# Stacked remainder rows in the product with V, other instruction orders in the attention blocks, and FFN input rows transposed on VectorE with six PSUM banks at the end of a pair

## The chip, the cores and the metric

The kernel runs on one core of one Trainium2 chip. The metric is the device time in microseconds of one launch. The kernel before takes 872.28 us (median of 3 runs, 872.03 to 872.45).

## The reference

A gated block of 2 x 2048 tokens of width 512: cross-attention to 77 context tokens per batch (16 heads of width 32), then an FFN of hidden width 1536 with integer weights, each behind a layer norm and a tanh gate. Cut to what matters:

```python
q = (layernorm(x) @ Wq.T);  k = ctx @ Wk.T;  v = ctx @ Wv.T          # 16 heads, 32 wide
scores = einsum('bhqd,bhkd->bhqk', q, k) * 32 ** -0.5
scores = where(arange(sq)[:, None] >= arange(77)[None, :], scores, -1e9)
x = x + tanh(g_xattn) * (softmax(scores) @ v) @ Wo.T
n = layernorm(x)
h = silu(n @ (w_gate / 127).T) * (n @ (w_up / 127).T)                 # 1536 wide
x = x + tanh(g_ffn) * h @ (w_down / 127).T
```

All arrays are fp32. The products run in fp32r with operands split into a high part (a copy rounded to fp32r) and a low part (the rest), so that a product of two split operands is three matmuls (high-high, low-high, high-low).

## The kernel before, in words

The 4096 rows are 8 blocks (`n`) of 512, each of 4 tiles (`t`) of 128 rows. Every engine has its own instruction list, written out by hand; semaphores alone tie the lists together, and nothing is reordered by a scheduler.

**Phase 1, attention.** A step handles one block. TensorE (PE) computes the queries transposed (`query`), per tile the scores (two units of 8 heads, 616 columns each, `score_unit`), transposes the probabilities (`transpose_p`, 10 transposes of 128 columns per tile, in three groups `r` of 4, 4 and 2), multiplies them with V (`values`, one block late), and projects with Wo (`project`). ScalarE (ACT) takes the exponentials (`exp0`, `exp1`) and writes the high parts (`p_high`, `m_high`, `x_high_t`); VectorE (DVE) takes maxima and sums, and writes the low parts (`p_low`, `m_low`); GpSimd (POOL) multiplies with the reciprocal denominators (`weigh`) and writes low parts of x (`x_low_t`). Loops over `n` are hardware loops. The 308 keys of a group of 4 heads are two chunks of 128 rows and a remainder of 52. In a unit of two groups the remainders lie side by side in one chunk of 104 rows, which both groups use, each with zero rows in V for the other. So a group has 3 chunks with 3 matmuls each: 9 matmuls of 512 columns, 4 groups per block.

**Phase 2, FFN.** Blocks go in 4 pairs (`p`). Gate and up projections of a pair are a Strassen-like scheme: for each of 12 slices `m` of the hidden width seven products `p1` to `p7` of 4 matmuls each (`strassen`, stationary operand from `ring`, moving operand from `xv`). The moving operands are the four quarters of the normalised, transposed input (B11, B12, B21, B22) and four differences T1 to T4. For pair 0 they are made at the end of phase 1. For every later pair they are made at the end of the pair before: PE transposes the rows (`turn`, 4 x 8 transposes) into PSUM, ACT rounds (`xv_copy`, `xv_high`), DVE forms differences and low parts (`form`, `xv_low`), POOL the low parts of T1 to T4. In each slice ACT snapshots partial sums from PSUM (`snap1` to `snap3`), takes tanh, and DVE makes silu of it (`silu1`, `silu2`) and the hidden values. POOL writes the low part of the hidden values (`h_low`). The down projection (`down`, 8 tiles of 12 matmuls) comes in two halves: the first after slice 6, the second at the pair's end. It writes two PSUM banks in turn (`m_bank`), and DVE adds each tile to `acc` (`result`). DVE takes row statistics and normalises the next pair's rows during the first half of the down projection (`first_half`). The last products of a pair are `p4(last)` and `p3(last)`, which wait for ACT's and DVE's treatment of `p7(last)`.

## Time and profile before

| what | us |
|---|---|
| median of 3 runs | 872.28 |
| the profiled execution, whole | 872.86 |
| its span | 871.0 |
| PE busy | 855.0 (98%) |
| DVE busy | 653.3 (75%) |
| ACT busy | 461.1 (53%) |
| POOL busy | 403.1 (46%) |

The granted TensorE clock stands at its full level in all 40 slices of the page. A row of a timeline names the start, the duration, the engine, the source line, the operation with output and inputs, its shape, and how many of them were merged. Matmuls overlap, so the pace of a run of matmuls is the distance from its start to the start of the next run, over its count, and not the mean duration. Idle time before a row stands in brackets, with what ended it.

### The profile page before, as it was taken

The numbers are of one execution on the slowest core, as the hardware profiler recorded it, in microseconds if no ns is written. First come the engines' busy times: TensorE is split into PE (matmuls) and PEld (weight loads), VectorE is DVE, ScalarE is ACT, GpSimd is POOL, SyncE is SP. The second block draws the span as 40 slices with busy tenths as digits, with TensorE's granted clock in tenths as the row PEclk, the third lists the DMA queues.
The fourth block names the chain that finished last, engine by engine and source line by source line (L and its number), as shares of the span: only waits on it lengthen the run. The fifth ranks groups of instructions, "written<-read, shape, count | busy, mean of one in ns | idle before, by whom it ended". The sixth has DMA issues, their size and how long they took to land.

```text
span 871.0 us, 12870 instructions
## 1 busy us (share of the span) xinstructions
PE 855.0 (98%) x4087; PEld 706.8 (81%) x4087; DVE 653.3 (75%) x1081; ACT 461.1 (53%) x1130; POOL 403.1 (46%) x344
## 2 busy tenths in 40 slices
PE   8999999999999999999999999999999999999997
PEld 6678888888888887888888888888888888888876
DVE  5988877777786878679688478788487887587882
ACT  5787575756666757546056265165363364461550
POOL 4664555555565665437144444155253256151250
PEclk9999999999999999999999999999999999999999
DMA  9233847272728131567333256043275143243202
GB/s 329 78 107 121 270 153 253 84 241 85 242 97 277 48 133 38 212 234 266 116 120 135 97 187 248 14 165 122 74 247 187 48 164 107 96 171 117 90 38 98
DMA packets 60406, 128.73 MB, mean 148 GB/s; under 512 B 7616, under 2 KB 20416, under 8 KB 60352
## 3 DMA queue, kind: packets, MB, share of 16 engines
q1 hardware_dynamic: 58960, 125.95, 41.9%
q10 hardware_dynamic: 1392, 2.10, 0.7%
q8 instruction: 29, 0.48, 0.2%
q14 instruction: 25, 0.20, 0.1%
HBM read 99.93 MB, written 27.79 MB: 147 GB/s over the span
## 4 chain that ended last, share of the span: by engine, by line
PE 86%; DVE 6%; ACT 3%; issue 1%; DMA 1%; POOL 1%; ACTq 0%; DVEq 0%
PE psum L1880 34%; PE psum L1591 20%; PE psum L1930 18%; PE psum L1660 9%; PE psum L1616 4%; DMA xs<-x_t 1%; PE psum L1704 1%; ACT e L800 1%; POOL hT L705 1%; DVE bn L1055 1%; DVE K L1149 1%; DVE mx L1105 1%; DVE e L1097 0%; DVE qT L1079 0%; DVE mx L1094 0%
## 5 line engine op out<-in xcount | busy, mean ns | idle before, releaser
L1880 PE MATMUL psum<-xv,ring 128*128 128x512 f32 x1344 | 308.0, 390 | 1.0 <-ACT a L985 0.7
L1880 PEld LDWEIGHTS psum<-xv,ring 128*128 128x128 f32 x1344 | 251.3, 188 | 55.1 <-ACT a L985 1.1
L705 POOL TENSOR_TENSOR hT<-th,hT 128x512 fp32r<-128x512 f32 x48 | 86.7, 1806 | 200.7 <-ACT hT L1005 200.7
L1930 PE MATMUL psum<-w_d,hT 128*128 128x512 f32 x768 | 177.7, 390 | 1.3 <-POOL hT L705 0.8
L1930 PEld LDWEIGHTS psum<-w_d,hT 128*128 128x128 f32 x768 | 143.6, 188 | 32.7 <-POOL hT L705 2.0
L554 POOL TENSOR_TENSOR e<-e,rden 128x616 f32<-128x616 f32 x64 | 78.0, 1219 | 110.4 <-DVE rden L1131 75.2
L800 ACT ACTIVATE e<-psum,nmx,q_scale 128x77 f32<-128x77 f32 x256 | 102.9, 428 | 3.1 <-DVE nmx L1111 3.1
L973 ACT ACTIVATE a<-psum 128x512 f32<-128x512 f32 x48 | 28.7, 599 | 131.6 <-PE psum L1880 131.4
L1471 DVE SCALAR_TENSOR_TENSOR acc<-psum,gate_ffn,acc 128x512 f32<-128x512 f32 x64 | 47.6, 749 | 65.1 <-PE psum L1930 65.1
L1660 PE MATMUL psum<-wo,aT 128*128 128x512 f32 x384 | 95.5, 398 | 0.5 <-DVE aT L1079 0.5
L1591 PE MATMUL psum<-xT,wq 128*128 128x512 f32 x360 | 89.1, 398 | 0.4 <-DVE qT L1079 0.4
L1660 PEld LDWEIGHTS psum<-wo,aT 128*128 128x128 f32 x384 | 69.8, 188 | 14.3 <-DVE aT L1079 0.8
L1591 PEld LDWEIGHTS psum<-xT,wq 128*128 128x128 f32 x360 | 65.5, 188 | 14.7 <-DVE qT L1079 1.9
L705 POOL TENSOR_TENSOR hT<-c,hT 128x512 fp32r<-128x512 f32 x48 | 62.3, 1297 | 22.2 <-ACT hT L1005 22.2
L1591 PE MATMUL psum<-pT,V 128*128 128x512 f32 x288 | 68.0, 392 | 0.6 <-DVE aT L1079 0.6
L773 ACT ACTIVATE pT<-psum 128x512 fp32r<-128x512 f32 (+1 forms) x96 | 49.7, 534 | 33.9 <-PE psum L1616 33.9
L1591 PE MATMUL psum<-K,qT 128*128 128x308 f32 x384 | 63.9, 310 | 0.9 <-ACT e L800 0.9
L1591 PEld LDWEIGHTS psum<-pT,V 128*128 128x128 f32 x288 | 53.3, 188 | 12.5 <-DVE aT L1079 1.1
L1435 DVE SCALAR_TENSOR_TENSOR th<-th,c 128x512 f32<-128x512 f32 x48 | 56.1, 1168 | 7.1 <-ACT th L998 4.3
L1591 PEld LDWEIGHTS psum<-K,qT 128*128 128x128 f32 x384 | 56.9, 188 | 5.4 <-ACT e L800 1.8
L1005 ACT ACTIVATE hT<-th 128x512 fp32r<-128x512 f32 x48 | 30.4, 633 | 54.2 <-DVE th L1448 54.2
L1068 DVE TENSOR_TENSOR pT<-psum,pT 128x512 fp32r<-128x512 f32 (+1 forms) x96 | 55.7, 588 | 2.6 <-ACT pT L773 0.9
(110 smaller groups left out, 1204.7 us busy)
## 6 DMA issues: line engine op xcount, KB each, us to landing
ring<-w_var SPq DMA_DIRECT2D x48, 896.0 KB, 4.6
w_var<-stage SPq DMA_DIRECT2D x12, 896.0 KB, 4.6
x_ln<-x SPq DMA_DIRECT2D x32, 256.0 KB, 4.7
x_res<-x SPq DMA_DIRECT2D x32, 256.0 KB, 5.2
x_mid<-x_res SPq DMA_DIRECT2D x32, 256.0 KB, 2.0
x<-x_mid SPq DMA_DIRECT2D x16, 512.0 KB, 5.6
acc<-x_mid SPq DMA_DIRECT2D x16, 512.0 KB, 6.2
out<-acc SPq DMA_DIRECT2D x32, 256.0 KB, 2.0
```

The lines of the kernel that those rows point to most:

```text
L554: nc.gpsimd.tensor_tensor(e[:, t % 2, hs], e[:, t % 2, hs], rden[:, t % 2, hs].unsqueeze(2).to_broadcast([P, UH, SK]), ALU.mult).then_inc( ...
L705: nc.gpsimd.tensor_tensor(hT[:, 1, i % HH, j, :], h[:, :], hT[:, 0, i % HH, j, :].bitcast(f32), ALU.subtract).then_inc(h_lo, 1)
L773: nc.scalar.activation(dst, src, ACT.Copy).then_inc(t_hi, 1)
L800: last = nc.scalar.activation(e[:, t % 2, UH + h, :], s_bank[1][:, h // HG, (h % HG) * SK:(h % HG + 1) * SK], ACT.Exp, bias=nmx[:, t % 2, ...
L1068: nc.vector.tensor_tensor(dst, src, hi.bitcast(f32), ALU.subtract).then_inc(t_free, 1)
L1435: nc.vector.scalar_tensor_tensor(th2[:, :], th2[:, :], 1.0, c22[:, :], ALU.add, ALU.mult)\
L1471: nc.vector.scalar_tensor_tensor(acc[:, t, :], m_bank[t % 2][:, :], gate_ffn[:, 0:1], acc[:, t, :], ALU.mult, ALU.add).then_inc(m_free, 1)
L1591: last = nc.tensor.matmul(dst, stat, mov, start=(j == 0), stop=(j == len(terms) - 1))
L1616: last = nc.tensor.transpose(t_bank[at % 2][:, j * P:(j + 1) * P], rows[:, start:start + P], ident[:, :])
L1660: last = nc.tensor.matmul(m_bank[t % 2][:, :], aT[:, a, m, t * P:(t + 1) * P], wo[:, c, m, :], start=m == 0 and a + c == 0, stop=m == G - ...
L1880: last = nc.tensor.matmul(psum[:, bank, :], stat, mov, start=start and j == 0, stop=j == len(terms) - 1, skip_group_check=not start)
L1930: last = nc.tensor.matmul(m_bank[t % 2][:, :], hT[:, a, m, t // TT, (t % TT) * P:(t % TT + 1) * P], w_d[:, HH * h + m, :], start=m == 0 an ...
```

## The change

**Attention.** A remainder of 52 rows is now kept in 64 partitions. The low part of the same rows goes to the other 64 partitions of the same operand `pR`, and V holds its remainder rows twice. One matmul with V's high part then does high-high and high-low, one with V's low part does the rest: 8 matmuls per group in place of 9. The transposes are regrouped: `r` = 0 and 1 are the four full chunks of unit 0 and of unit 1, `r` = 2 the two remainders. For `r` = 2 ACT and DVE have two instructions on 64 partitions each in place of one on 128. The orders of ACT, DVE and POOL within a step are others. All four groups' remainder matmuls wait for the last low part of the block before (`t_base(n)`).

**FFN.** For pairs 1 to 3 PE transposes nothing. POOL normalises the rows in slices 2, 3 and 5; DVE takes the statistics in slices 1 to 4 and transposes the rows in 32 instructions per pair (`turn_rows`, each 16 blocks of 32 x 32, all from one group of 32 partitions into another), of which 20 lie between the results of the first half of the down projection (`FILL`), 3 ahead of them and 9 in slices 7 to 9. The differences and low parts read SBUF in place of PSUM; T1 and T3 are formed in slices 10 and 11. ACT computes Silu itself, and DVE's `silu1` and `silu2` are gone. At a pair's end the second half of the down projection uses six PSUM banks (the two of `m_bank` and four of the products'), and `p4(last)` and `p3(last)` stand between parts of its first three tiles. The row maxima of the weights (`largest_gu`) are all taken in the last pair, where before 6 slices' were taken in the first.

`values_full` waits for `t_free` of `split - 2 + m // 2` and has 2 chunks of 3 matmuls; `values_rest` waits for `split` and has the 2 matmuls with `pR`. The two loops over `odd` are those of `p_high` and `p_low` for `r` = 2.

```diff
-    SH = 2 * (GK - 2 * P)
-    CS = [0, P, 2 * P, 2 * P + SH, 3 * P + SH]
+    HP = P // 2
+    CS = [0, P, GK - HP, HK - 2 * P, HK - P]
...
             def values(i, m, b, split):
-                pe.wait_ge(t_free, split)
-                m_wait(i)
-                product(m_bank[m % 2][:, :],
-                        [(V[:, B - 1 - b, a, 3 * m + c, :], pT[:, d, CU * (m // 2) + 2 * (m % 2) + c, :])
-                         for c in range(3) for a, d in CROSS]
-                        ).then_inc(m_full, 1)
+                values_full(i, m, b, split)
+                values_rest(m, b, split)
...
+                for odd in range(2):
+                    rows = slice(odd * HP, odd * HP + HP)
+                    last = nc.scalar.activation(pR[rows, :, odd, c], src[rows], ACT.Copy)
...
+                for odd in range(2):                                              # p_low, r = 2
+                    last = nc.vector.tensor_tensor(pR[other, :, odd, c], src[rows], pR[rows, :, odd, c].bitcast(f32),
+                                                   ALU.subtract)
...
+            def turn_rows(q, half_of, ops):
+                tiles = slice(TT * half_of, TT * half_of + TT)
+                dve.wait_ge(x2_normed, PT * q + TT * (half_of + 1))
...
+                for op in ops:
+                    a, c = divmod(op, HG)
+                    rows = x2[a * HD:(a + 1) * HD, tiles, :].rearrange("p t (k n) -> p t k n", n=P)
+                    to = x2_t[half_of][c * HD:(c + 1) * HD].rearrange("p k (t n) -> p t k n", n=P)
+                    nc.vector.transpose(to[:, :, :, a * HD:(a + 1) * HD], rows[:, :, :, c * HD:(c + 1) * HD])\
+                        .then_inc(x2_turned, 1)
...
-                nc.scalar.activation(th1[:, :], psum[:, set_a[i % 2], :], ACT.Tanh, scale=0.5 * W_SCALE)\
-                    .then_inc(tanh1_done, 1)
+                nc.scalar.activation(th1[:, :], psum[:, set_a[i % 2], :], ACT.Silu, scale=W_SCALE)\
+                    .then_inc(silu1_done, 1)
...
+            def down_bank(h, t):
+                bank = {2: set_c[0], 3: set_b[1], 4: set_c[1], 5: set_a[1]}
+                return psum[:, bank[t], :] if h and t in bank else m_bank[t % 2][:, :]
...
-                if more:
-                    turn(p + 1, B11)
-                    turn(p + 1, B12)
+                early, late = range(HH - 2), range(HH - 2, HH - 1)
+                down(p, 1, 0, early)
                 p4(last)
+                down(p, 1, 1, early)
                 p3(last)
-                down(p, 1, 0, range(HH - 1))
-                down(p, 1, 1, range(HH - 1))
+                down(p, 1, 2, early)
+                for t in range(3):
+                    down(p, 1, t, late)
```

PE's instructions at the end of a pair that is not the last, of the kernel before. L1880 are the Strassen products, L1704 the transposes of `turn`, L1930 the down projection:

```order
L1930 MATMUL psum<-w_d,hT 128x512 x96
L1880 MATMUL psum<-xv,ring 128x512 x140
L1704 MATMUL psum<-ident,x 128x128 x16
L1880 MATMUL psum<-xv,ring 128x512 x8
L1930 MATMUL psum<-w_d,hT 128x512 x24
L1704 MATMUL psum<-ident,x 128x128 x16
L1930 MATMUL psum<-w_d,hT 128x512 x72
```

The same place of the changed kernel, where L1982 are the products and L2042 the down projection:

```order
L2042 MATMUL psum<-w_d,hT 128x512 x96
L1982 MATMUL psum<-xv,ring 128x512 x140
L2042 MATMUL psum<-w_d,hT 128x512 x8
L1982 MATMUL psum<-xv,ring 128x512 x4
L2042 MATMUL psum<-w_d,hT 128x512 x8
L1982 MATMUL psum<-xv,ring 128x512 x4
L2042 MATMUL psum<-w_d,hT 128x512 x80
```

The 32 transposes are gone, and 8 matmuls of the down projection stand ahead of each of the last two products.

DVE's instructions in the second part of the first half of the down projection, of the kernel before: L1471 is `result`, L1257 and L1259 are the statistics, L1265 the normalisation, L1421 and those behind it belong to the next slice:

```order
L1471 SCALAR_TENSOR_TENSOR acc<-psum,gate_ffn,acc 128x512
L1257 BN_STATS bn<-x 128x6
L1259 BN_AGGR mv<-bn 128x2
L1471 SCALAR_TENSOR_TENSOR acc<-psum,gate_ffn,acc 128x512
L1265 TENSOR_SCALAR x<-x,mv,rstd 128x512 x2
L1257 BN_STATS bn<-x 128x6
L1259 BN_AGGR mv<-bn 128x2
L1471 SCALAR_TENSOR_TENSOR acc<-psum,gate_ffn,acc 128x512
L1265 TENSOR_SCALAR x<-x,mv,rstd 128x512 x6
L1421 TENSOR_TENSOR c<-psum,a 128x512
L1435 SCALAR_TENSOR_TENSOR th<-th,c 128x512
L1441 SCALAR_TENSOR_TENSOR th<-th,psum 128x512
```

And of the changed kernel, where L1567 is `result` and L1362 `turn_rows`:

```order
L1567 SCALAR_TENSOR_TENSOR acc<-psum,gate_ffn,acc 128x512
L1362 STREAM_TRANSPOSE x_t<-x 32x4x4x32 x2
L1567 SCALAR_TENSOR_TENSOR acc<-psum,gate_ffn,acc 128x512
L1362 STREAM_TRANSPOSE x_t<-x 32x4x4x32 x3
L1567 SCALAR_TENSOR_TENSOR acc<-psum,gate_ffn,acc 128x512
L1362 STREAM_TRANSPOSE x_t<-x 32x4x4x32 x3
L1529 TENSOR_TENSOR c<-psum,a 128x512
L1544 TENSOR_TENSOR th<-th,c 128x512
```

Between two results two or three transposes have taken the place of one statistic and, at the end, the normalisations; the two silu instructions of each slice are gone.

## Rows read from the trace of the kernel before

**Rows 1.** The page, its first part: busy time, share, instructions.
```profile
PE 855.0 (98%) x4087; PEld 706.8 (81%) x4087; DVE 653.3 (75%) x1081; ACT 461.1 (53%) x1130; POOL 403.1 (46%) x344
```

**Rows 2.** Timeline of PE in a middle step: start, us, line, operation, count.
```profile
230.25 2.12 PE L1591 MATMUL psum<-K,qT 128*128 128x308 f32 x12
232.21 8.36 PE L1591 MATMUL psum<-pT,V 128*128 128x512 f32 x36
240.40 1.85 PE L1591 MATMUL psum<-K,qT 128*128 128x308 f32 x12
...
272.13 2.11 PE L1591 MATMUL psum<-K,qT 128*128 128x308 f32 x12
```

**Rows 3.** Timeline of PE at the end of pair 1.
```profile
592.12 1.91 PE L1704 MATMUL psum<-ident,x 128*128 128x128 f32 x16
593.78 2.08 PE L1880 MATMUL psum<-xv,ring 128*128 128x512 f32 x8
595.70 4.70 PE L1930 MATMUL psum<-w_d,hT 128*128 128x512 f32 x20
600.65 1.21 PE L1930 MATMUL psum<-w_d,hT 128*128 128x512 f32 x4 [0.26 <-POOL hT L705]
601.70 1.91 PE L1704 MATMUL psum<-ident,x 128*128 128x128 f32 x16
603.37 16.62 PE L1930 MATMUL psum<-w_d,hT 128*128 128x512 f32 x72
619.82 42.91 PE L1880 MATMUL psum<-xv,ring 128*128 128x512 f32 x188
```

**Rows 4.** Timeline of PE in the last pair.
```profile
786.52 21.93 PE L1930 MATMUL psum<-w_d,hT 128*128 128x512 f32 x96
808.29 31.90 PE L1880 MATMUL psum<-xv,ring 128*128 128x512 f32 x140
840.88 1.20 PE L1880 MATMUL psum<-xv,ring 128*128 128x512 f32 x4 [0.69 <-ACT a L985]
...
849.64 16.61 PE L1930 MATMUL psum<-w_d,hT 128*128 128x512 f32 x72 [0.50 <-DVE acc L1471]
```

**Rows 5.** Groups by form: line, engine, form, count, busy, mean ns, idle before.
```profile
L1068 DVE TENSOR_TENSOR pT<-psum,pT 128x256 fp32r<-128x256 f32 x32 | 13.5, 421 | 1.7 <-ACT pT L773 0.2
L773 ACT ACTIVATE pT<-psum 128x256 fp32r<-128x256 f32 x32 | 13.1, 411 | 0.9 <-PE psum L1616 0.9
L1149 DVE TENSOR_TENSOR K<-psum,K 32x154 fp32r<-32x154 f32 x16 | 5.0, 312 | 0.2
L1068 DVE TENSOR_TENSOR pT<-psum,pT 128x512 fp32r<-128x512 f32 x64 | 43.0, 672 | 0.9 <-ACT pT L773 0.7
L1265 DVE TENSOR_SCALAR x<-x,mv,rstd 128x512 f32<-128x512 f32 x24 | 11.4, 541 | 0.0
L1435 DVE SCALAR_TENSOR_TENSOR th<-th,c 128x512 f32<-128x512 f32 x48 | 56.1, 1168 | 7.1 <-ACT th L998 4.3
L1448 DVE TENSOR_TENSOR th<-th,c 128x512 f32<-128x512 f32 x48 | 33.6, 700 | 1.7
L750 ACT ACT_TABLE_LOAD x1 | 1.3, 1283 | 4.6 <-issue 4.6
```

**Rows 6.** Timeline of DVE, pair 1, first half of the down projection.
```profile
544.25 0.75 DVE L1471 SCALAR_TENSOR_TENSOR acc<-psum,gate_ffn,acc 128x512 f32<-128x512 f32 x1 [1.15 <-PE psum L1930]
...
546.97 0.75 DVE L1471 SCALAR_TENSOR_TENSOR acc<-psum,gate_ffn,acc 128x512 f32<-128x512 f32 x1 [1.15 <-PE psum L1930]
...
561.24 2.82 DVE L1265 TENSOR_SCALAR x<-x,mv,rstd 128x512 f32<-128x512 f32 x6
```

**Rows 7.** Timeline of DVE, the end of a middle step.
```profile
231.11 1.01 DVE L1068 TENSOR_TENSOR pT<-psum,pT 128x512 fp32r<-128x512 f32 x2
```

**Rows 8.** Timeline of PE, the last attention step.
```profile
332.56 1.11 PE L1591 MATMUL psum<-K,qT 128*128 128x308 f32 x6 [0.42 <-ACT e L800]
```

More of the change, by code:

```diff
@@ L393, in residual @@
                     sp.dma_start(x_res[:, t, :], x_f[n - 1, :, t, :]).then_inc(res_in[t], 16)
-                if ahead and not first:
+                if rows_ahead:
+                    sp.wait_ge(xb_full, nth(TURNED, 0, B21))
+                    for j in range(TT):
+                        load_x2(1, j)
+                if ahead:
                     load_x(n + 2)
@@ L454, in pair @@
             def pair(p):
+                if 0 < p < NP - 1:
+                    sp.wait_ge(xv_lo, nth(LO_ORDER, p, T4))
+                    for j in range(TT):
+                        load_x2(p + 1, j)
                 for m in range(MH):
@@ L1521, in pair @@
                         hidden2(i - 1)
[L1522 removed]
+                    if p == NP - 1:
                         largest_gu(i)
+                    if more and 1 <= m <= TT:
+                        for t in (2 * m - 2, 2 * m - 1):
+                            stats2(2 * p + 2 + t // TT, t % TT)
+                    if more and m == HH:
+                        turns(p + 1, range(FILL[0]))
+                    if more and HH < m < HH + 4:
+                        at = (23, 26, 29, 32)[m - HH - 1:m - HH + 1]
+                        turns(p + 1, range(at[0], at[1]))
+                    if more and m == MH - 2:
+                        form(p + 1, T1)
+                    if more and m == MH - 1:
+                        form(p + 1, T3)
                 gate2(last)
[L1525 removed]
                 if more:
                     xv_low(p + 1, B11, b11_at)
[L1528 removed]
                 hidden1(last)
@@ L1611, in transpose_p @@
                 rows = e[:, t % 2].rearrange("p h k -> p (h k)")
-                first, parts = P_PARTS[r]
-                for j in range(parts):
-                    u, c = divmod(first + j, CU)
-                    start = u * HK + CS[c]
+                starts = [r * HK + CS[c] for c in FULL] if r < 2 else [u * HK + CS[CU // 2] for u in range(2)]
+                for j, start in enumerate(starts):
                     last = nc.tensor.transpose(t_bank[at % 2][:, j * P:(j + 1) * P], rows[:, start:start + P],
@@ L1864, in _ @@
             last_step(NB - 1, B - 1)
-            for m in range(G):
-                values(M_LAST + m, m, B - 1, T_P2 - 2 + min(m, 2))
-                if m == 1:
-                    turn(0, B22)
-            turn(0, B21)
+            for m in range(2):
+                values_full(M_LAST + m, m, B - 1, T_P2)
+            for m in range(2):
+                values_rest(m, B - 1, T_P2)
+            turn(B22)
+            for m in range(2, G):
+                values(M_LAST + m, m, B - 1, T_P2)
+            turn(B21)
             pe.wait_ge(m_free, M_LAST + 4)
```

528 lines of the change are left out of this document (289 added, 239 removed).

## The prediction

> **What bounds the kernel now.** I read the page's first part, then PE's timeline from start to end, then the groups by form, then DVE's timeline where the change puts work. The first part shows PE busy in 98% of the span and DVE in 75% [rows 1]. So what counts is what PE issues, and at which pace. In a middle step nothing stops it: 36 products with V go from 232.21 to 240.40, 8.19 us or 0.2275 us each, with 12 score products on either side, and the step repeats after 272.13 - 230.25 = 41.88 us [rows 2]. In the FFN 96 down-projection matmuls take 808.29 - 786.52 = 21.77 us, 0.2268 each [rows 4]. The reader is to see that the kernel has almost no waits to remove in its long stretches, so a gain must come from fewer PE instructions, and that the exceptions are the ends of the pairs.
>
> **Products with V.** 8 blocks x 4 groups lose one matmul each: 32 x 0.2275 = 7.3 us [rows 2]. The number of transposes of P stays at 10 per tile. What could take this back is the new wait: the remainder matmuls of group 0 need the last low part of the block before. In the middle step DVE writes the last two low parts of P until 231.11 + 1.01 = 232.12, and the products start at 232.21 [rows 2, 7]. Now the last one comes in two halves on ACT and two on DVE. A half with 256 columns costs what the whole did, 0.42 on DVE and 0.41 on ACT [rows 5], and instructions on part of the partitions are no cheaper by row (32 partitions x 154 columns: 0.312) [rows 5]. So the last low part is done some 0.7 to 0.8 us later, at about 232.9. The 6 matmuls of full chunks stand ahead of the remainder, 6 x 0.2275 = 1.37 us, so it starts at 233.6. The wait is covered, with about 0.7 us left.
>
> Behind that, each tile costs ACT and DVE about 0.35 us more, 1.4 us per step on each. Queued behind the late halves are DVE's next maxima, and the exponentials wait for those. I take 0.1 us per step for slips, 0.7 us over seven steps, bounds 0 and 1.3 us per step (four tiles with the whole 0.33 on the path, against the 0.9 us that a step gains). The new orders may remove the few waits of early steps; I give this 0.5 us, bounds 0 and 1.2. In the last step there are no queries to cover the softmax chain, and PE already waits for the exponentials of the tile before (0.42 at 332.56) [rows 8]. There ACT's second half of `r` = 2 stands between one tile's exponentials and the next one's: three times 0.33 us, 1.0 us lost, bounds 0 and 1.3.
>
> **Transposes at the pairs' ends.** 16 of them go from 592.12 to 593.78, 1.66 us, 0.104 each [rows 3]. Three pairs x 32 x 0.104 = 10.0 us that leave PE.
>
> **The rest of a pair's end.** From 592.12 to 619.82 PE takes 27.70 us for 104 matmuls (8, 20, 4 and 72) and 32 transposes [rows 3]. The matmuls at pace are 104 x 0.2268 = 23.6, the transposes 3.3, so 0.8 us are slow starts and the wait of 0.26 for the low hidden values. Three ends: 2.3 us. In the new order 8 down matmuls, 1.81 us, stand where 16 transposes of 1.66 us covered ACT's and DVE's answer to `p7(last)`, and 8 more ahead of `p3(last)`. DVE no longer has a silu in the chain from `p4(last)` to the low hidden values, but ACT has a rounding of 1024 columns in it. With 8 + 4 + 8 + 6 matmuls (5.9 us) between `p4(last)` and the first use of slice 11's low part, I count the whole 0.8 as gone.
>
> In the last pair nothing covers that answer now: from 808.29 to 849.64 PE takes 41.35 us for 172 matmuls (140, then 4 + 4 + 20 + 4), 39.0 at pace. 0.1 us is a transpose that stays, so 2.2 us are waits, 0.69 and 0.50 of them in brackets [rows 4]. The same new order covers them: 2.2 us.
>
> **What is added off PE.** The trace has no DVE transpose. One moves 512 elements per partition from SBUF to SBUF. From below, a normalisation of 512 columns takes 0.47 back to back (6 in 2.82) [rows 6]. From above, the dearest 512-column row is 1.168, an operation that reads two SBUF operands beside POOL's work [rows 5]. The nearest rows are 0.67 and 0.70 for 512 columns with little overlap [rows 5]; I take 0.70, since partition changes should stop them from overlapping. The Trainium skill, "VectorE: DVE Perf Modes", section "The three transpose paths", gives 311 ns for 128 columns in bf16; an estimate from that with one element per cycle for the other 384 is 0.71, which no run here has shown. Its "Rules for kernel authors" send a 128 x 128 transpose to TensorE, which speaks against this change; the trace prices TensorE's at 0.104 us of the bound engine [rows 3].
>
> Between two results PE has 12 matmuls, 2.72 us. DVE has one result of 0.75 [rows 6] and 2.5 transposes on average, 1.75: 2.5 us in all. It just fits, and the wait in brackets of 1.15 before each result [rows 6] shrinks to about 0.2. The break-even is (2.72 - 0.75) / 2.5 = 0.79 us per transpose. In slices 7 to 9 DVE has five operations of 0.70 and three transposes, 5.6 us of the 28 x 0.2268 = 6.35 that PE needs. The two silu operations that go (1.17 and about 0.7) more than pay for that. At the pair's end the forms and low parts that now read SBUF lie behind the last five tiles, 13.6 us, in which DVE has five results (3.8 us) and four operations of 1024 elements, each at most two of 0.70 (5.6 us). So 96 x 0.70 = 67 us on DVE cost nothing. POOL, busy in 46% [rows 1], takes 24 normalisations. Silu in place of tanh is one more table load, on ACT in pair 0's slice 1: 1.28 us [rows 5], on an engine that is busy in 53% of the span [rows 1]; I take 0.3, bounds 0 and 1.3. The skill's "ScalarE: Activation LUTs", section "What ACT_TABLE_LOAD costs", adds a drain of about 1.4 us, which would make it 1 us; the trace shows the load with its number and no drain.
>
> **Sum.** -7.3 - 10.0 - 2.3 - 2.2 - 0.5 + 0.7 + 1.0 + 0.3 = -20.3 us. The profiled execution took 872.86 us whole for a span of 871.0, so it becomes a span of 850.7 and 852.6 whole. It lay 0.6 above the median of 872.28; against that median I predict 852.0 us.
>
> **Rivals.**
> - *Attention eats its share.* DVE's and ACT's added halves lie on the path in every tile: 7 steps lose up to 1.3 us each in place of 0.1, so 852.0 + 8.4 = 860.4; half of it is 856. For it: DVE has the least room of all helpers there. Against it: in a middle step PE never waited, and over the run only 0.9 us of DVE's idle stands before low parts of P [rows 5], which says that ACT is usually ahead.
> - *DVE's transposes are dearer and PE stalls on `m_bank`.* From 0.79 us on, a pair loses 8 x (0.75 + 2.5 T - 2.72). At T = 0.95 this is 3.2 us, three pairs 9.7: 861.7.
> - *Slower than before.* Same mechanism: 32-bit transposes at half rate or with a stop per 32 x 32 block, T near the upper row of 1.17. Then also slices 7 to 9 are too long: 3 x (3.5 + 3 T - 6.35). A pair loses 7.6 + 2.0 = 9.6 us, and three lose 28.8: 880.8. It decides from about T = 1.07, where a pair loses the 6.8 us that equal the gain. For it: the trace has no such operation and one 512-column SBUF operation at 1.17. Against it: that one is dear by its second SBUF operand.
> - *No waits at all come in.* Then the sum is -7.3 - 10.0 - 2.3 - 2.2 - 1.2 = -23.0: 849.3.
>
> **Chances.** Forecast with its own range of 849 to 855: 0.68. Attention's share lost: 0.13. Dearer transposes: 0.10. Slower: 0.05. Anything else, a late load of the next rows at a pair's start among it: 0.04. The range that leaves out no more than 2 in 10 is 848.5 to 860. A difference of 0.2%, 1.7 us, is about what a measurement of this kernel can tell from none. Faster by more: 0.92; the same: 0.02; slower: 0.06.
>
> **What would show it.** Right: PE has 256 products with V at 0.2275 us, middle steps of about 41.0 us, no transposes of the rows on PE after the first pair's, no idle at 8 + 4 + 8 + 4 matmuls of a pair's end, and a pair of 528 x 0.2268 = 119.7 us. DVE's transposes take 0.65 to 0.75 us and its results still wait for PE. Wrong: results of the first half of the down projection that start late with PE idle behind `result`; score products that wait for exponentials in every tile; or a first matmul of `values_rest` that starts more than 0.1 us behind its forerunner. The prediction fails above all if one DVE transpose costs more than 0.8 us.

## The result and the profile after

| | before | after |
|---|---|---|
| median (lowest to highest), us | 872.37 (872.03 to 872.48), 4 runs | 858.17 (857.34 to 858.99), 4 runs |
| ratio after/before | | 0.9837, 95% interval 0.9825 to 0.9848 |
| span and whole time of the profiled execution, us | 871.0, 872.86 | 857.1, 858.88 |

The kernel is 1.6% faster. The forecast was 852.0 with a range of 848.5 to 860.0: the time lies inside, 6.2 us above the forecast, and outside the narrower 849 to 855 to which the prediction gave 0.68. PE is still what bounds it. First part of the page of the kernel after (busy time, share, instructions):

```profile
PE 838.4 (98%) x3959; PEld 692.0 (81%) x3959; DVE 681.9 (80%) x1089; ACT 471.1 (55%) x1160; POOL 415.8 (49%) x374
```

DVE took on 28.6 us of work and PE lost 16.6 [rows 1]. Where the 13.9 us of span went is seen in PE's starts: the first score product of each attention step, and the first product of the FFN.

| PE, us | before | after | difference | priced |
|---|---|---|---|---|
| step 1 | 42.22 | 45.37 | +3.15 | -0.8 |
| step 2 | 42.74 | 40.90 | -1.84 | -0.8 |
| steps 3, 4, 5 | 125.97 | 122.81 | -3.16 | -2.4 |
| step 6 | 41.52 | 41.42 | -0.10 | -0.8 |
| last step | 58.19 | 59.12 | +0.93 | -0.7 |
| FFN, to the end of the span | 499.2 | 486.3 | -12.9 | -14.2 |

The new orders, priced at 0.5 over all steps, stand in no row of the last column. So the miss is in the attention: it gained 1.0 us where 6.1 were priced (the 5.5 of the column and the 0.5 of the orders; the differences add to 1.02). Three steps lose it: step 1 is 4.0 us over its price, the last step 1.7, step 6 0.7. Step 2 came out 1.0 better than its price, steps 3 to 5 together 0.8. The FFN is 1.3 us over.

A middle step does what was forecast. PE's timeline, the step that answers to [rows 2] (start, us, line, operation, count):

```profile
229.37 2.11 PE L1693 MATMUL psum<-K,qT 128*128 128x308 f32 x12
231.32 1.53 PE L1753 MATMUL psum<-pT,V 128*128 128x512 f32 x6
232.69 0.62 PE L1761 MATMUL psum<-pR,V 128*128 128x512 f32 x2
...
238.81 1.85 PE L1693 MATMUL psum<-K,qT 128*128 128x308 f32 x12
...
270.25 2.11 PE L1693 MATMUL psum<-K,qT 128*128 128x308 f32 x12
```

32 products take 238.81 - 231.32 = 7.49 us where 36 took 8.19, and the step takes 40.88 us where it took 41.88. So 0.7 us of the 1.0 lie in the products, at 0.234 us each and not the 0.2275 of the price. Most of the rest lies in the stretch of the queries to the next step's start (12.35 us, where it was 12.72). No brackets stand here: the remainder products find their halves in time.

In pair 1 the transposes are gone from PE, and the two places with work of p3 and p4 between down products have no wait. Timeline of PE, which answers to [rows 3]:

```profile
588.41 1.99 PE L2042 MATMUL psum<-w_d,hT 128*128 128x512 f32 x8
590.23 1.08 PE L1982 MATMUL psum<-xv,ring 128*128 128x512 f32 x4
591.15 1.99 PE L2042 MATMUL psum<-w_d,hT 128*128 128x512 f32 x8
592.97 1.08 PE L1982 MATMUL psum<-xv,ring 128*128 128x512 f32 x4
593.89 18.31 PE L2042 MATMUL psum<-w_d,hT 128*128 128x512 f32 x80
612.03 42.94 PE L1982 MATMUL psum<-xv,ring 128*128 128x512 f32 x188
```

And DVE in the first half of the down projection, which answers to [rows 6]. The wait before a result was 1.15 us; now it is 0.23 or none, with 2 or 3 transposes of 0.70 to 0.72 us between results:

```profile
545.77 0.75 DVE L1567 SCALAR_TENSOR_TENSOR acc<-psum,gate_ffn,acc 128x512 f32<-128x512 f32 x1
546.55 1.44 DVE L1362 STREAM_TRANSPOSE x_t<-x 32x512 f32<-32x512 f32 x2
548.23 0.75 DVE L1567 SCALAR_TENSOR_TENSOR acc<-psum,gate_ffn,acc 128x512 f32<-128x512 f32 x1 [0.23 <-PE psum L2042]
549.01 2.17 DVE L1362 STREAM_TRANSPOSE x_t<-x 32x512 f32<-32x512 f32 x3
```

Step 1 is where the profile shows a new stall. PE, DVE and GpSimd there:

```profile
68.79 2.06 PE L1753 MATMUL psum<-pT,V 128*128 128x512 f32 x6 [1.99 <-DVE aT L1155]
```
```profile
65.41 1.82 DVE L1194 SCALAR_TENSOR_TENSOR nmx<-mx,q_scale,minus 128x8 f32<-128x8 f32 x1
...
68.07 0.66 DVE L1155 TENSOR_TENSOR aT<-psum,aT 128x512 fp32r<-128x512 f32 x1
```
```profile
63.70 3.50 POOL L609 TENSOR_TENSOR V<-v_late,V 128x1536 fp32r<-128x1536 f32 x1 [3.71 <-ACT V L806]
```

`nmx` (the offset of the exponentials, made from the maxima) is an operation on 8 columns that took 0.23 us at this place before. Here it lasts until 67.23, and GpSimd's subtraction until 67.20. PE waits 1.99 us for what DVE does behind it, the low part of the product with V (`aT`). After that wait PE's granted clock is low. The view by windows (window, length, busy time and count of PE, PEld, DVE, ACT, POOL, then the clock, DMA share, GB/s):

```profile
66.00:69.00 3.00, 1.01 (x5) 0.55 (x4) 2.85 (x5) 2.51 (x11) 1.20 (x1) 1.00 0.11 34
69.00:72.00 3.00, 3.00 (x10) 2.36 (x10) 2.70 (x8) 1.87 (x10) 1.78 (x2) 0.64 0.89 258
72.00:75.00 3.00, 3.00 (x14) 2.54 (x13) 0.72 (x3) 0.97 (x3) 1.85 (x2) 0.79 1.00 342
75.00:80.00 5.00, 5.00 (x32) 4.39 (x31) 4.71 (x10) 4.44 (x14) 0.00 (x0) 1.00 0.53 157
```

A mean of 0.64 is time at both levels, 1.2 and 2.4 GHz. From 69 to 75 PE loses 3 x 0.36 + 3 x 0.21 = 1.7 us by it, and from 75 it has the high clock again. The four timed runs of this kernel have 857.1 and 857.2 us of span at a mean clock of 0.997, and 855.6 and 855.7 at 0.999, so the fall is worth about 1.5 us and does not come every time. Differences below that are read from the traces.

### The profile page after: what moved, and what is told of

Its sections match the earlier page's. It is cut to its first block, busy times and chain, and to the rows that moved or that the text cites. A ratio compares the mean times of both kernels' runs of the same rounds, so it can differ in the third digit from the quotient of the medians.

```text
span 857.1 us, 12731 instructions
## 1 busy us (share of the span) xinstructions
PE 838.4 (98%) x3959; PEld 692.0 (81%) x3959; DVE 681.9 (80%) x1089; ACT 471.1 (55%) x1160; POOL 415.8 (49%) x374
## 4 chain that ended last, share of the span: by engine, by line
PE 81%; DVE 8%; SPq 3%; ACT 3%; DMA 2%; issue 2%; POOL 1%; ACTq 0%; DVEq 0%
PE psum L1982 33%; PE psum L2042 20%; PE psum L1693 11%; PE psum L1774 8%; PE psum L1753 5%; SPq L461 3%; PE psum L1716 3%; PE psum L1761 1%; ACT e L850 1%; DMA gates<-g_ffn 1%; DVE x_t L1362 1%; DMA x_ln<-x 1%; DVE mx L1188 1%; DVE pT L1135 1%; DVE bn L1122 1%
## 5 line engine op out<-in xcount | busy, mean ns | idle before, releaser
L1982 PE MATMUL psum<-xv,ring 128*128 128x512 f32 x1344 | 309.4, 390 | 0.5 <-DVE c L1538 0.5
L1982 PEld LDWEIGHTS psum<-xv,ring 128*128 128x128 f32 x1344 | 251.4, 188 | 55.9 <-DVE c L1538 1.7
L2042 PE MATMUL psum<-w_d,hT 128*128 128x512 f32 x768 | 177.0, 389 | 0.0
L2042 PEld LDWEIGHTS psum<-w_d,hT 128*128 128x128 f32 x768 | 144.2, 188 | 30.1
L742 POOL TENSOR_TENSOR hT<-th,hT 128x512 fp32r<-128x512 f32 x48 | 71.6, 1492 | 187.8 <-ACT hT L1072 187.8
L1040 ACT ACTIVATE a<-psum 128x512 f32<-128x512 f32 x48 | 28.7, 598 | 112.8 <-PE psum L1982 112.8
L1693 PEld LDWEIGHTS psum<-xT,wq 128*128 128x128 f32 x360 | 65.8, 188 | 13.9 <-DVE qT L1155 0.9
L1362 DVE STREAM_TRANSPOSE x_t<-x 32x512 f32<-32x512 f32 x96 | 67.4, 702 | 2.9
L1567 DVE SCALAR_TENSOR_TENSOR acc<-psum,gate_ffn,acc 128x512 f32<-128x512 f32 x64 | 46.6, 747 | 26.1 <-PE psum L2042 25.8
L1544 DVE TENSOR_TENSOR th<-th,c 128x512 f32<-128x512 f32 x48 | 36.4, 758 | 31.7 <-ACT th L1058 31.7
L1052 ACT ACTIVATE a<-psum 128x512 f32<-128x512 f32 x48 | 28.7, 598 | 57.8 <-PE psum L1982 57.8
L850 ACT ACTIVATION_READ_ACCUMULATOR e<-psum,nmx,q_scale 128x1 f32 x256 | 55.0, 215 | 0.0
L1559 DVE TENSOR_TENSOR c<-c,th 128x512 f32<-128x512 f32 x48 | 50.2, 1046 | 5.0
L815 ACT ACTIVATE pT<-psum 128x512 fp32r<-128x512 f32 x64 | 36.4, 607 | 32.3 <-PE psum L1716 32.2
```

The costliest lines, as they stand in the source:

```text
L742: nc.gpsimd.tensor_tensor(hT[:, 1, i % HH, j, :], h[:, :], hT[:, 0, i % HH, j, :].bitcast(f32), ALU.subtract).then_inc(h_lo, 1)
L815: nc.scalar.activation(dst, src, ACT.Copy).then_inc(t_hi, 1)
L850: last = nc.scalar.activation(e[:, t % 2, UH + h, :], s_bank[1][:, h // HG, (h % HG) * SK:(h % HG + 1) * SK], ACT.Exp, bias=nmx[:, t % 2, ...
L1362: nc.vector.transpose(to[:, :, :, a * HD:(a + 1) * HD], rows[:, :, :, c * HD:(c + 1) * HD])\
L1559: nc.vector.tensor_tensor(c12[:, :], c12[:, :], th2[:, :], ALU.mult).then_inc(h2_done, 1)
L1567: nc.vector.scalar_tensor_tensor(acc[:, t, :], down_bank(h, t), gate_ffn[:, 0:1], acc[:, t, :], ALU.mult, ALU.add).then_inc(m_free, 1)
```

## Experiments

Each is the changed kernel with the edit shown, timed beside the kernel before (871.8 to 873.8 us in all these runs), unless it says otherwise.

### V's high rows early again

```diff
                 p(2, 2)
+                v_high(1)
                 q(2)
...
                 p(3, 2)
-                v_high(1)
```

> The changed kernel with one edit: on ScalarE, V's high rows of block 1 (v_high(1)) go back ahead of q(2), where they stood before the change. My theory, from the trace of the changed kernel: their later place moves GpSimd's V low rows (L609, 3.50 us) from 60.5 to 63.70, so that VectorE's nmx (L1194) of step 1 takes 1.82 us instead of 0.23 and TensorE stands idle 66.64 to 68.79, after which its granted clock is low for some 8 us; step 1 costs 45.37 us instead of 42.22. Undone, step 1 comes back to 42 to 43 us and the time falls by 2.5 to 4 us, to 854 to 856. Rival: the step lost its time because the new order of step 1 puts more work ahead of the first row of V on VectorE wherever V comes, and then the time stays within 0.5 us of 858.2. A second rival: the copy stands in the way of q(2) on ScalarE and its 1.5 us show in step 1 instead: a gain of 1 to 2 us only.

858.29 us, ratio 0.9832 (0.9816 to 0.9849): no gain. The theory was half right. `nmx` was short again, but the stall moved ahead of it. ACT and PE in this run:

```profile
58.57 1.49 ACT L806 ACTIVATE V<-v_late 128x1536 fp32r<-128x1536 f32 x1 [1.54 <-DMA v_late<-v_keys]
```
```profile
62.05 0.44 PE L1716 MATMUL psum<-ident,e 128*128 128x128 f32 x2 [2.00 <-DVE pT L1135]
```

ScalarE waited 1.54 us for the DMA of `v_late`, and `q(2)`, queued behind it, came late. In the kernel before, the same copy started at 56.99 without a wait. The view of the tile `v_late` says why, of before and of after (last columns: first and last start):

```profile
L424 SPq DMA_DIRECT2D v_late<-v_keys x12: 764/843/876, 44.2 to 53.7; - x12
```
```profile
L461 SPq DMA_DIRECT2D v_late<-v_keys x14: 763/837/876, 45.2 to 56.5; - x14
```

The remainder rows of V are stored twice now, once for each half of the partitions. That is two issues more for each half of V, 28 in a row instead of 24 on SP's queue at some 0.87 us each, so the last one starts 2.8 us later (56.5 instead of 53.7). My prediction counted the matmuls that stacking saves and the halves that it rounds, and no issue on SP.

### V's low rows in pieces

```diff
-                nc.gpsimd.tensor_tensor(V[:, B - 1 - b, 1], v_full[b][:, :, :], ...)
+                for k in range(0, NV, 2):
+                    last = nc.gpsimd.tensor_tensor(V[:, B - 1 - b, 1, k:k + 2], v_full[b][:, k:k + 2, :], ...)
```

> The changed kernel with one edit: GpSimd's V low rows (L609, one subtraction of 128x1536 in 3.50 us) are done as six subtractions of 128x256. My theory says that a VectorE instruction with two operands from SBUF is held until the subtraction that GpSimd has under way is over: nmx (L1194) took 1.82 us and ended with L609. With pieces of about 0.6 us it is held for at most one piece, so nmx takes 0.3 to 0.8 us, the idle time of TensorE in step 1 (2.06 us) shrinks by 1 us or more, and the time falls by 1 to 3 us, to 855 to 857. Rival: the two engines share one path at half speed each, so that the length of GpSimd's instructions does not matter: nmx still takes over 1.2 us, and the time stays within 0.5 us or grows by up to 0.5 us for the five more starts.

856.27 us, 0.9815 (0.9799 to 0.9832). The six pieces took 4.23 us in all, and `nmx` 0.45 us beside them. DVE's and PE's rows:

```profile
66.02 0.45 DVE L1196 SCALAR_TENSOR_TENSOR nmx<-mx,q_scale,minus 128x8 f32<-128x8 f32 x1
```
```profile
68.03 1.65 PE L1755 MATMUL psum<-pT,V 128*128 128x512 f32 x6 [0.63 <-DVE aT L1157]
```

PE's wait fell from 1.99 to 0.63 us, and its clock stayed at 1.00 in every window from 57 to 110 us. The length of GpSimd's instruction decided, not its sum, so the rival of a path shared at half speed falls.

### V's high rows behind q(2)

```diff
                 q(2)
+                v_high(1)
                 p(3, 0)
...
-                v_high(1)
```

> The changed kernel with one edit: on ScalarE, V's high rows of block 1 stand between q(2) and p(3,0). With them ahead of q(2) (the run before) the 2 us of idle time did not go: ScalarE sat 1.54 us until v_late was there (58.57), q(2) came late behind it, TensorE waited 2.00 us at 62.05 and its granted clock fell to 0.59 and 0.84 in the next 6 us. My theory now: what is late is V itself. Its rows come in 14 DMA issues a half instead of 12, some 0.87 us each, so v_late is whole at 58.6 instead of before 57.0, and any place of the copy that is early waits for it, any late one pushes GpSimd's V low rows onto VectorE's nmx. Behind q(2) the copy starts at 58.6 as well, in time in which ScalarE is idle (57.67 to 59.49), delays p(3,0) by 0.5 to 0.6 us, and GpSimd is done with V at 63.7, ahead of nmx at 65.4: TensorE's longest wait in step 1 is 0.5 to 1.4 us, its clock stays at 1.00, and the time falls by 1.5 to 3.5 us, to 854.7 to 856.7. Rival: the delay of p(3,0) adds to the wait that is there (0.80 at 60.87) and with over 1.3 us the clock falls again: within 0.7 us of 858.2.

856.60 us, 0.9820 (0.9804 to 0.9837), in the range of my theory. The copy started at 59.10, GpSimd was done at 64.15, `nmx` took 0.22 us at 66.39. PE's longest wait was 1.31 us, at 61.85 just ahead of the step, and the clock held at 1.00.

### Two of V's issues on another queue

With `v_high(1)` ahead of `q(2)` and the last step's new order (below):

```diff
-                for odd, c, j, row, key, rows in V_PLACES:
+                load_v(sp, b, V_PLACES[2 * b:])
...
                 exp0(0, 1)
+                act.wait_ge(v_zero, B)
+                load_v(act, 1, V_PLACES[0:1])
                 p(0, 2)
+                load_v(act, 1, V_PLACES[1:2])
                 exp1(0, 2)
```

> The changed kernel with V's high rows of block 1 back ahead of q(2) on ScalarE (alone no gain: 858.29), the new order of the last attention step (alone 857.44), and two of the 14 DMA issues of v_late moved from SP's queue to ScalarE's, into gaps of 0.59 and 0.43 us that it has at 42 and 43 us. No pieces on GpSimd. It asks whether V's lateness is what cost step 1 its time. SP's 28 issues in a row take 24.6 us, some 0.87 each; two fewer make v_late whole at about 56.9 instead of 58.57. My theory: ScalarE then has no wait of 1.54 before the copy, q(2) comes as before the change, nmx is free of GpSimd, no idle time of TensorE in step 1 is over 1.2 us, its granted clock stays at 1.00, and step 1 takes 41.3 to 42.5 us instead of 45.37 (and of 42.54 with the pieces). Time 854.2 to 855.5. Rival: ScalarE has no room for the two issues at 42 us, what follows shifts, and the 1.5 us of the copy ahead of q(2) show as such: 855.8 to 857.5. If V's lateness were not the cause, nothing would be gained over the last step's 0.7: 857.4.

855.16 us, 0.9804 (0.9791 to 0.9818), the lowest time of all. The two issues took 1.75 and 0.79 us on ScalarE's queue, more than its gaps, without harm that the trace shows. ACT's copy now:

```profile
57.13 1.49 ACT L810 ACTIVATE V<-v_late 128x1536 fp32r<-128x1536 f32 x1
```

No wait before the copy, `nmx` at 0.22 us, the clock at 1.00 throughout, and the step takes 103.45 - 61.24 = 42.21 us instead of 45.37. PE's longest waits are 0.83 us just ahead of the step and 0.41 in it. Against the run with the copy early (858.29) this is 3.1 us, of which the last step's order is worth 0.7: so with the copy ahead of `q(2)`, V's late arrival cost 2.4 us, the clock's fall included. It is not the only cause in the changed kernel, where the copy stands late by its new place (62.1), while the two runs that wait for V have it by 58.6 and 59.1: behind `q(2)`, with no DMA touched, the copy regains 1.6 us. The early place costs time because V is late, the late place because GpSimd then meets `nmx`. The step is still 1.3 us longer than a middle one, and 0.8 over its price.

### The last attention step's order on VectorE

```diff
                 for t in range(1, TT):
-                    largest1(n, t)
-                    offset1(n, t)
+                    if t == 1:
+                        largest1(n, t)
+                        offset1(n, t)
...
                     p(n, t - 1, 2)
+                    if t + 1 < TT:
+                        largest1(n, t + 1)
+                        offset1(n, t + 1)
                     p(n, t, 0)
```

> The changed kernel with one edit: in the last attention step VectorE does the largest value and the offset of the next tile ahead of this tile's probabilities and residual, not behind them. My theory: the last step's period grew from 6.51 to 7.27 us per tile (where I had priced 0.33 a tile) because the rounding of the probabilities in two halves, on ScalarE 0.77 and on VectorE 0.86, stands twice in the loop from one tile's exponentials to the next tile's: exp, high part, low part, largest, offset, exp. With largest and offset ahead the loop loses VectorE's half: the period falls to 6 to 6.5 us and the time by 1.5 to 3 us, to 855 to 856.7. Rival: the step is bound by GpSimd's sum of the halves (the waits of 0.57 and 1.42 us for e, L590) or by ScalarE's own queue, and reordering VectorE moves nothing: within 0.5 us of 858.2, or slower by up to 1 us, where the probabilities come later than now.

857.44 us, 0.9822 (0.9805 to 0.9840): by the medians a difference of 0.7 us, too small to tell. By the traces the last step is shorter. In the kernel after, its rows on DVE and PE read (period 337.67 - 330.40 = 7.27, where before it was 6.51):

```profile
338.30 0.86 DVE L1148 TENSOR_TENSOR pR<-psum,pR 64x256 fp32r<-64x256 f32 x2 [0.44 <-ACT pR L831]
...
339.79 0.74 DVE L1232 SCALAR_TENSOR_TENSOR x_res<-psum,gate_t,x_res 128x512 f32<-128x512 f32 x1
340.45 0.79 DVE L1188 TENSOR_REDUCE mx<-psum 128x8 f32<-128x616 f32 x1
```
```profile
330.40 1.11 PE L1693 MATMUL psum<-K,qT 128*128 128x308 f32 x6 [0.42 <-ACT e L850]
...
337.67 1.11 PE L1693 MATMUL psum<-K,qT 128*128 128x308 f32 x6 [0.42 <-ACT e L850]
343.86 0.66 PE L1716 MATMUL psum<-ident,e 128*128 128x128 f32 x4 [1.42 <-POOL e L590]
```

The maximum of the next tile, on which its exponentials wait, stood behind both halves, a transposed tile and a residual. With the edit it starts at 338.64 instead of 340.45. The products of `wo` start at 359.19 instead of 359.73, in a run that was 0.2 us behind at 318 us: 0.7 us gained of the 1.5 that this loop had lost (from the first scores of tile 1 to the first rows for the FFN PE takes 347.10 - 322.27 = 24.83 us; before it took 347.73 - 324.42 = 23.31). The wait of 1.42 shrank to 0.36, but one of 1.04 for DVE's `pT` came in at 333.91.

### The two gains together

The pieces and the last step's order, and both with the copy behind `q(2)`.

> The changed kernel with two edits that each brought something: V's low rows on GpSimd in six pieces (alone 856.27) and the new order of the last attention step on VectorE (alone 857.44). They lie 240 us apart, so the gains should add: 858.2 less 1.9 less 0.7, 855.3 to 856.0. Rival: the first gain moves the clock's fall to another place, and the sum is no better than 856.3.

> The changed kernel with three edits: V's high rows of block 1 behind q(2) on ScalarE (alone 856.60), V's low rows in six pieces, the new order of the last attention step. The first two fight the same stall: with the copy behind q(2) nmx is free of GpSimd in any case, and the wait of 1.31 us before p(3,0)'s products stays. So no better than with the pieces alone: 855.3 to 856.4. Rival: with the copy early the pieces let VectorE's neighbours through as well, and it gives 0.5 us more, under 855.3.

855.41 us, 0.9806 (0.9793 to 0.9820), and 855.63 us, 0.9810 (0.9797 to 0.9824). The two edits add. The third gives nothing on top, as I expected, since it serves the same stall. The mean clock was 0.999 or more each time, so the clock's fall did not move elsewhere.

### The orders of the kernel before

Stacked rows and FFN as changed; on VectorE, ScalarE and GpSimd the attention steps 1 to 6 in their old order. Three lines of ScalarE's as an example:

```diff
-                x_high_t(n + 1, 0)
-                weighted(n, 0)
                 exp0(n, 0)
+                weighted(n, 0)
```

> The changed kernel, its stacked rows and its FFN kept, with the orders of the kernel before in the attention steps 1 to 6 on VectorE, ScalarE and GpSimd (V's high rows of block 1 ahead of q(2) too). I had priced the new orders at 0.5 us in all. By the run with V's copy back alone, step 1 is no better for it. My theory: 858.2 to 860.5, the whole steps 3 to 5 up to 0.3 us longer each with a wait or two of TensorE that the new orders do not have. Rival: the order of the kernel before fits the stacked rows badly, since the half-height rounding (0.77 on ScalarE, 0.86 on VectorE) stands ahead of exponentials and rows of V: every step is over 1 us longer and the time is above 864. A second rival: the new orders cost (they put a transposed tile ahead of the exponentials) and without them the time is under 857.5.

879.95 us, 1.0084 (1.0069 to 1.0100): 21.8 us slower than the changed kernel and slower than the kernel before. The first rival was right and my theory was not. Every step has waits like these; PE in a middle one:

```profile
223.41 0.44 PE L1697 MATMUL psum<-ident,e 128*128 128x128 f32 x2 [0.61 <-DVE pT L1123]
...
232.90 0.44 PE L1697 MATMUL psum<-ident,e 128*128 128x128 f32 x2 [0.99 <-DVE pT L1123]
```
```profile
226.90 0.86 DVE L1136 TENSOR_TENSOR pR<-psum,pR 64x256 fp32r<-64x256 f32 x2 [0.44 <-ACT pR L828]
...
228.86 0.75 DVE L1220 SCALAR_TENSOR_TENSOR x_res<-psum,gate_t,x_res 128x512 f32<-128x512 f32 x1
229.52 0.79 DVE L1158 TENSOR_REDUCE mx<-psum 128x8 f32<-128x616 f32 x1
```

A tile takes 232.90 - 223.41 = 9.49 us, where it takes 8.3 in the kernels before and after. By the order of the rows it is the loop of the last step again: halves on ScalarE (226.09), halves on VectorE (226.90), statistics, a residual, and only then the maximum (229.52) that the next exponentials need. In the kernel after, the maxima of tile 2 follow the halves at once (247.44, then 248.33), with the statistics and the residual elsewhere; for tile 3 one residual stands between, and no statistics. The step takes 44.5 us instead of 40.9. Three engines' orders changed at once, and which move counts was not separated. The orders of the kernel before without stacked rows take 859.19 us (the next run), so under these orders stacking by itself costs 20.8 us. The new orders without stacked rows were not run.

### The FFN alone

The kernel before in its attention (rows of each head apart, old orders), the FFN of the changed kernel.

> The kernel before in its attention steps (remainder rows of each head by themselves, the old orders on all engines), with the FFN of the changed kernel (transposes on VectorE, six banks, Silu). By the two traces the FFN went from 494.1 to 481.5 us, 12.6 less: the time should be 859.3 to 860.3. What is then left for stacked rows and orders is 1.0 to 2.1 us, of 6.8 that I had counted (7.3 + 0.5 less 0.7 and less 0.3 for the table load, which is in the FFN, plus the last step's 1.0). Rival: a part of the FFN's gain hangs on the attention's new orders (where rows and loads of the first pair stand), and alone it gives under 11 us: over 861.

859.19 us, 0.9852 (0.9835 to 0.9868), 13.4 us less than the 872.63 us of the kernel before beside it. That is the FFN's whole share, and stacking with its orders has 1.0 us left, as the table of steps says (-1.02).

### Two banks at a pair's end

```diff
-            return psum[:, bank[t], :] if h and t in bank else m_bank[t % 2][:, :]
+            return m_bank[t % 2][:, :]
...
-                down(p, 1, 0, early)
                 p4(last)
-                down(p, 1, 1, early)
                 p3(last)
-                down(p, 1, 2, early)
```

> The changed kernel with one edit: at a pair's end p4 and p3 run first, and all products of the second half of down go through the same two PSUM banks, with no interleaving, as in the kernel before. Transposes stay on VectorE. My theory: the six banks are worth what I counted for them, 2.2 us in the last pair and 2.3 in each of the three others (where the slow starts after TensorE's transposes are gone, only the waits are left, so 1.5 to 2.3), 7 to 9 us in all: 865 to 867. Rival: the transposes off TensorE are by themselves enough to remove the waits at the end of pairs 0 to 2, and the banks serve the last pair alone: 860.4.

872.22 us, 1.0000 (0.9991 to 1.0010): 14.0 us slower than the changed kernel, where my theory had 7 to 9, and as slow as the kernel before, though its transposes stay on VectorE. PE at the end of pair 1:

```profile
591.83 1.20 PE L1982 MATMUL psum<-xv,ring 128*128 128x512 f32 x4 [0.69 <-ACT a L1052]
593.73 1.21 PE L1982 MATMUL psum<-xv,ring 128*128 128x512 f32 x4 [0.70 <-DVE c L1538]
...
600.81 13.94 PE L2036 MATMUL psum<-w_d,hT 128*128 128x512 f32 x60 [0.39 <-DVE acc L1567]
615.83 3.02 PE L2036 MATMUL psum<-w_d,hT 128*128 128x512 f32 x12 [1.08 <-DVE acc L1567]
```

A pair takes 124.46 us (494.22 to 618.68). The kernel before took 123.97 (495.85 to 619.82) and the changed one takes 120.42. The waits in brackets are 2.9 us a pair. The transposes on PE had covered the answer of ScalarE and VectorE; taken away alone, they leave waits of their size. The ScalarE and VectorE orders at the pair's end were left as they are for six banks, so a part of the 14 us may be theirs; that was not separated.

### More transposes between results

All 32 in the first half of the down projection, four to a result:

```diff
-            FILL = (3, 5, 7, 10, 12, 15, 17, 20, 23)
+            FILL = tuple(range(0, 33, 4))
```

> The changed kernel with one edit: all 32 transposes on VectorE of a pair stand in the first half of down and none in slices 7 to 9, four to each of its eight results instead of three or two. My theory, the break-even sum of the prediction: between two results TensorE has 2.72 us of work, VectorE 0.75 us of its own and four transposes of 0.70 to 0.72, together 3.6 us, so TensorE waits 0.85 to 0.9 us at each of eight results, 6.8 to 7.2 us in a pair and 20 to 21.5 us in three pairs, less some 1.5 us that slices 7 to 9 win: 876 to 878, slower than the kernel before. Rival: the two banks and hT's products take up much of it and the wait is under 0.4 us a result: under 868.

And the 9 of slices 7 to 9 as 1, 4, 4 instead of 3, 3, 3:

```diff
-                        at = (23, 26, 29, 32)[m - HH - 1:m - HH + 1]
+                        at = (23, 24, 28, 32)[m - HH - 1:m - HH + 1]
```

> The changed kernel with one edit: of the 32 transposes on VectorE per pair, the 9 that stand in slices 7 to 9 of the down projection as 3, 3, 3 stand there as 1, 4, 4. My theory: the 0.31 us wait of TensorE in slice 8 of each of three pairs comes from the three transposes (2.17 us) that follow a hidden product (L1559) of 1.79 us, lengthened beside GpSimd's own product; with one transpose there the wait is gone and the time falls by 0.6 to 0.9 us (3 x 0.2 to 0.3), to about 857.4. Rival: four transposes in the next slices (2.9 us) are late for their own product in turn: no change, or up to 1 us slower.

All in down: 872.84 us, 0.9998 (0.9988 to 1.0007), 14.7 slower than the changed kernel, less than the 18 to 20 that I expected. DVE and PE:

```profile
549.40 0.75 DVE L1567 SCALAR_TENSOR_TENSOR acc<-psum,gate_ffn,acc 128x512 f32<-128x512 f32 x1
550.19 2.90 DVE L1362 STREAM_TRANSPOSE x_t<-x 32x512 f32<-32x512 f32 x4
553.12 0.75 DVE L1567 SCALAR_TENSOR_TENSOR acc<-psum,gate_ffn,acc 128x512 f32<-128x512 f32 x1
```
```profile
553.92 3.04 PE L2042 MATMUL psum<-w_d,hT 128*128 128x512 f32 x12 [0.68 <-DVE acc L1567]
557.65 3.06 PE L2042 MATMUL psum<-w_d,hT 128*128 128x512 f32 x12 [0.69 <-DVE acc L1567]
...
574.08 3.24 PE L1982 MATMUL psum<-xv,ring 128*128 128x512 f32 x13 [1.63 <-ACT a L1052]
```

VectorE's period is 553.12 - 549.40 = 3.72 us against PE's 2.72, as the break-even sum says. But PE starts with two free banks and waits only behind the fifth product, and VectorE carries the rest of its debt into the next slice, where PE waits 1.63.

The 1, 4, 4 gave 862.02 us, 0.9874 (0.9857 to 0.9890), 3.8 slower where I had expected a gain; about 3 of them are left when runs of like mean clock are compared (860.32 against 857.34 and 857.47 at 0.999). The stall of 0.16 in slice 8 went, and two came, 0.46 and 0.30 in brackets, where four transposes in a row (2.90 us) hold up `c` (L1538); a pair takes 121.2 us instead of 120.4.

## Why the prediction was right, and what it missed

- **Price and place of VectorE's transposes: right.** I took 0.70 us; the row reads 702 ns for 96 of them, far from the break-even of 0.79. At 2 or 3 between results they cost nothing; the rivals by price are out. Row of the kernel after, by form:

```profile
L1362 DVE STREAM_TRANSPOSE x_t<-x 32x512 f32<-32x512 f32 x96 | 67.4, 702 | 2.9
```

- **FFN -14.2: came out at -12.9 in the span, -13.4 by the run of the FFN alone.** The sum holds, its terms do not stand alone: I gave the transposes 10.0 and the pair's new end 4.5, but without that end the transposes give nothing (872.22). Missing are about 0.3 us at each of three slices 8 (PE 435.80 to 446.09 for 44 products, 10.29 where 10.0 is the pace), and 0.4 in the first block (414.03 - 370.79 = 43.24, where it took 42.81 before). I had priced the table load that stands there at 0.3. That the load makes the whole 0.4 was not tested. The drain that the Trainium skill ("ScalarE: Activation LUTs", section "What ACT_TABLE_LOAD costs") adds to a load is not in the trace: the load begins 0.01 us behind the instruction ahead of it, which ends at 377.25, and ScalarE goes on 0.02 us behind the load:

```profile
377.26 1.28 ACT L1065 ACT_TABLE_LOAD   x1
378.56 0.63 ACT L1065 ACTIVATE th<-c 128x512 f32<-128x512 f32 x1
```

- **Slice 8: the step that failed was "in slices 7 to 9 DVE has five operations of 0.70".** One of them, the product with two SBUF operands (L1559), took 1.79 us beside GpSimd's product, and the three transposes behind it came late. GpSimd's row, then VectorE's, in pair 1:

```profile
561.67 1.29 POOL L742 TENSOR_TENSOR hT<-th,hT 128x512 fp32r<-128x512 f32 x1 [19.89 <-ACT hT L1072]
```
```profile
561.72 1.79 DVE L1559 TENSOR_TENSOR c<-c,th 128x512 f32<-128x512 f32 x1
```

  The 1024-column forms at the pair's end, which I gave at most two of 0.70, took 1.7 to 3.4 us each, and hid behind PE as forecast.
- **Products with V: right where the step is steady.** Steps 3 to 5 gained 1.05 us each against 0.81 priced, 0.7 of it in the products (0.91 was the price) and most of the rest in a stretch that the price did not touch. The halves are in time, as forecast.
- **Step 1: the failed step is "lose one matmul each" as the whole cost of stacking outside ScalarE and VectorE.** The layout asks for four more DMA issues, and the new orders move V's copy. Step 1 took 4.0 us more than its price: 3.2 of them go with the copy early and two issues off the queue, which frees the copy, `nmx` and the clock at once, and 0.8 stay (two of the four issues stay too). By the run with the copy early and no issue moved, the issues alone cost 2.4 us at that place.
- **The new orders, "0.5, bounds 0 and 1.2": the worst-sized term.** With stacked rows they are worth 21.8 us. For the waits of early steps alone the term was not far off: step 2 gained 1.0 us beyond its price. I read them as polish on the old schedule, while they are what lets the halves fit. The term for slips (0.1 a step) came out right in the middle steps only because of them.
- **The last step: the term of 1.0 was too small, and the products saved hardly show.** It priced the second half of ScalarE alone (0.33 a tile). Two halves take 0.77 us on ScalarE and 0.86 on VectorE where the whole took 0.41 and 0.42, the two stand in one loop, and each of the last two tiles grew by 0.76 us (6.51 to 7.27), 1.5 in all. The loop is bound by more than the order of the maxima: moving them gave back only 0.7. That is 0.5 of the 1.7 us. The larger part, 1.2, is that eight products fewer (1.8 us) shortened the two stretches that hold them by 0.17 (10.77 to 10.60) and 0.42 (24.11 to 23.69) only. Part of it is a longer wait for `aT` between the groups, before and after:

```profile
320.19 4.39 PE L1591 MATMUL psum<-pT,V 128*128 128x512 f32 x18 [0.34 <-DVE aT L1079]
```
```profile
318.28 1.62 PE L1753 MATMUL psum<-pT,V 128*128 128x512 f32 x6 [0.81 <-DVE aT L1155]
```

  The low part of `aT` for which PE waits there is done 6.46 us after the step's start, where before it was 6.39, so fewer products ahead of it are a longer wait. No run was made on it.
- **Rival "attention eats its share" (860.4): nearly its number, not its mechanism.** It put the loss into every tile; middle steps lost nothing. The place was step 1, the last step and step 6. That the time fell inside the wide range owes something to luck: its upper part was there for this rival and for dearer transposes, neither of which came, and the FFN carried 13 of the 14 us.
- **Open:** step 6 gained 0.1 us where 0.8 was due, with a wait of PE of 0.38 us for VectorE's residual (L1232) ahead of 293.88; no run was made on it. Steps 1 and 6 are the two in which VectorE takes eight row statistics and not four, and step 1 has such a wait too (0.22 at 88.42); that these are connected is not shown.

## What to carry to other kernels

When a layout stores something twice, count the DMA issues too, and follow the queue that makes them to the first reader: here they cost 2.4 us with the copy at its old place, a third of what the saved products were priced at. A change that adds work between two exponentials and the order that makes room for it are one thing, and a price for either alone misleads; the same holds for work taken from the bound engine where that work had covered another engine's answer. If a stall moves when its first cause is mended, ask what both places wait for.

## What the runs showed of the hardware

- **A small VectorE operation can last as long as GpSimd's large one.** `nmx`, 8 columns and all its operands in SBUF, took 1.82 us and ended within 0.03 us of GpSimd's subtraction of 3.50 us; it took 0.22 us with GpSimd idle and 0.45 beside pieces of 0.75 us. The product of 512 columns that began 0.05 us after GpSimd's (561.67 + 1.29 = 562.96) ended 0.55 us behind it, at 563.51. Operations with an operand in PSUM ran beside the same subtraction at their usual time (0.79 us for a maximum). The Trainium skill, "SBUF — State Buffer", section "Who interferes with whom", says that a VectorE instruction with two SBUF inputs and a GpSimd instruction that reads SBUF take turns on a shared pair of ports, each holding it for its whole length. The traces agree, and the pieces show it by an edit.
- **TensorE's granted clock fell in most traces after an idle time of about 2 us in step 1, and not after 1.31 (copy behind q(2)) or 0.80 (pieces, the longest there).** After 1.99 us it read 0.64 and then 0.79 for three microseconds each (the changed kernel), after 2.00 us 0.59 and 0.84 (copy early). It does not always fall: in the trace of the run with two banks the same idle time of 1.98 us left it at 1.00. Over the seven kernels that keep this stall, 22 of 40 timed runs had a mean clock of 0.998 or less; over the five that shorten it, none of 23. So a stall of 2 us cost up to 3.7.
